# A decoder block on one core: self-attention's products, some copies and loads in another order

## What is computed

```python
# x: 4 x 512 x 128, ctx: 4 x 154 x 128, mask: 4 x 1 x 512 x 154
def attn(x, Wk, Wq, Wv):                      # one head of 128, causal
    scores = (x @ Wq) @ (x @ Wk)^T / sqrt(128), later keys at -inf
    return softmax(scores) @ (x @ Wv)

def xattn(q, kv, mask, ...):                  # 16 heads of 8, over the 154 rows of ctx
    scores = query @ key^T / sqrt(8), masked
    return (softmax(scores) @ value) @ wo + bo

def ffn(x, ...):                              # self-attention with rope, then experts
    q, k, v = x @ Wq + bq, x @ Wk + bk, x @ Wv + bv        # 16 heads of 8
    q, k = q * cos + rotate_half(q) * sin, k * cos + rotate_half(k) * sin
    ao = softmax(q @ k^T / sqrt(8)) @ v                    # 512 x 512 scores per head
    x1 = layernorm(x + ao @ Wo + bo) * g1 + be1
    p, i = top 2 of softmax(x1 @ Wg + bg) of 8 experts, p made to sum to 1
    y = sum of p * (gelu(x1 @ W1[i] + b1[i]) @ W2[i] + b2[i])   # hidden 512
    return layernorm(x1 + y) * g2 + be2

x = x + attn(layernorm(x), ...)
x = x + xattn(layernorm(x), ctx, mask, ...)
x = x + ffn(layernorm(x), ...)
```

## Time and profile before

| | us |
|---|---|
| median of 3 runs | 740.26 |
| lowest, highest | 740.03, 741.62 |
| the profiled execution | 746.73 |
| its span, first to last instruction | 744.9 |
| PE, DVE, ACT, POOL busy in the span | 645.0, 453.8, 344.4, 121.6 |

### The profile page before, as it was taken

One profiled execution on the slowest core, in us unless ns is written; L12 is line 12 of the kernel. 1 busy time (PEld: TensorE's weight loads), 2 busy tenths in 40 slices (PEclk: granted clock), 3 DMA queues, 4 the chain that ended last, 5 costly groups with the idle time before them and its releaser, 6 DMA issues.

```text
span 744.9 us, 10652 instructions
## 1 busy us (share of the span) xinstructions
PE 645.0 (87%) x3806; PEld 401.2 (54%) x3814; DVE 453.8 (61%) x1119; ACT 344.4 (46%) x617; POOL 121.6 (16%) x121
## 2 busy tenths in 40 slices
PE   4799899998898899999898899999888999886950
PEld 2563554456646653478536653388446643475950
DVE  4673777736836677467726578667534688377303
ACT  0405127663054567754235467754344476632620
POOL 5100100001143000010405100030406000224014
PEclk9999999999999999999899999999999999997985
DMA  6300000001053540012353430020354600126851
GB/s 193 109 0 1 1 0 1 1 1 36 4 176 95 143 110 1 1 35 80 101 153 84 131 99 1 1 76 18 102 149 125 170 20 0 29 65 201 255 143 42
DMA packets 45083, 54.95 MB, mean 74 GB/s; under 512 B 4346, under 2 KB 35432, under 8 KB 45032
## 3 DMA queue, kind: packets, MB, share of 16 engines
q1 hardware_dynamic: 43240, 50.61, 23.6%
q0 software_dynamic: 1792, 3.67, 1.6%
HBM read 46.73 MB, written 7.54 MB: 73 GB/s over the span
## 4 chain that ended last, share of the span: by engine, by line
PE 66%; DVE 18%; issue 5%; ACT 5%; DMA 2%; POOL 2%; SPq 1%; POOLq 0%; ACTq 0%; DVEq 0%
PE banks L1712 8%; PE banks L1680 6%; PE banks L1359 6%; PE banks L1373 5%; PE banks L1336 5%; PE banks L1702 4%; DVE nm L1192 3%; DVE nm L1128 3%; PE banks L1663 3%; PE banks L1607 2%; PE banks L1605 2%; PE banks L1624 2%; PE banks L1618 2%; DVE hat L886 1%; PE banks L1430 1%
## 5 line engine op out<-in xcount | busy, mean ns | idle before, releaser
L1192 DVE TENSOR_REDUCE nm<-banks 128x1 fp32r<-128x512 f32 x256 | 159.9, 684 | 43.4 <-PE banks L1680 43.2
L839 ACT ACTIVATE px<-banks 128x1024 f32<-128x1024 f32 x128 | 125.5, 1023 | 41.3 <-PE banks L1702 40.9
L667 ACT ACTIVATE hT<-banks,wp 128x128 f32<-128x128 f32 x240 | 68.3, 368 | 84.6 <-PE banks L1359 79.9
L559 POOL TENSOR_TENSOR rstd<-ve,misc 128x4 f32<-128x4 f32 x19 | 19.5, 1027 | 473.7 <-DVE ve L880 473.7
L1359 PE MATMUL banks<-xT,wp 128*128 128x128 f32 x480 | 70.0, 292 | 14.2 <-DMA wp<-in_experts 7.9
L1359 PEld LDWEIGHTS banks<-xT,wp 128*128 128x128 f32 x480 | 62.7, 203 | 21.0 <-issue 12.8
L1680 PE MATMUL banks<-kst,qst 32*128 32x512 f32 x256 | 70.7, 474 | 2.4 <-DVE nm L1192 1.4
L1373 PE MATMUL banks<-wp,hT 128*128 128x128 f32 x480 | 68.1, 288 | 2.1 <-ACT hT L667 2.1
L1712 PE MATMUL banks<-px,vf 128*32 128x512 f32 x512 | 68.2, 604 | 1.4 <-ACT px L839 0.7
L1336 PE MATMUL banks<-sel_r,eye_r 128*128 128x512 f32 x168 | 64.6, 463 | 5.0 <-DVE nm L1192 4.0
L1373 PEld LDWEIGHTS banks<-wp,hT 128*128 128x128 f32 x480 | 62.9, 203 | 3.6 <-ACT hT L667 2.6
(11 more groups left out here) (273 smaller groups left out, 997.5 us busy)
## 6 DMA issues: line engine op xcount, KB each, us to landing
wp<-in_experts SPq DMA_DIRECT2D x60, 514.0 KB
b2r<-in_L_ffn_b SPq DMA_DIRECT2D x60, 64.0 KB
expert_rows<-xs SPq DMA_DIRECT2D x12, 256.0 KB, 4.4
xs<-expert_tokens SPq DMA_DIRECT2D x9, 256.0 KB, 2.9
msk<-in_mask SPq DMA_DIRECT2D x4, 308.0 KB, 3.2
xin<-in_x SPq DMA_DIRECT2D x4, 256.0 KB, 2.9
ot<-in_const_sel SPq DMA_DIRECT2D x1, 1024.0 KB, 5.1
out<-yg SPq DMA_DIRECT2D x4, 256.0 KB, 2.4
```

What stands on the lines that cost most here:

```text
L667: ins = act.activation(hT[:, n % 2, c * P:(c + 1) * P], bank[h_bank(p, i)][:, c * P:(c + 1) * P], ACT.Gelu, bias=wp[:, n % WSLOTS, 2 * FF ...
L839: act.activation(px[:, c % 2, 2 * i:2 * i + 2, :], banks[:, 4 + 2 * i:6 + 2 * i, :], ACT.Exp, scale=SCALE_H).then_inc(k["f_exp"], 1)
L1192: dve.tensor_reduce(nm[:, t, g, BLK * hh:BLK * hh + 1], bank[s1_bank(g, t, hh)], AX.X, ALU.max, negate=True).then_inc(k["f_max"], 1)
```

## The change

1. Self-attention: the four `s1` of a query tile come in the order of heads 2, 3, 0, 1 (`HEADS_IN_TURN`), so that the two beside `s2` of heads 0 and 1 use the other rows of the array, and those beside `s2` of heads 2 and 3 too. The value sums move from behind the second `s2` to between the halves of a step (behind everything in a group's last step, or when no `s1` is left, which is as before for the latter). The keep-warm product before each `q2` is gone (16 in all).
2. Tail: VectorE normalises `xa` before the sum with o_proj, and makes klo before the moments of batch n (`keys_low`, split from `keys_values`); TensorE turns the rows before expert td, and makes the query projection before expert te; ScalarE's copies move with them (hatT before gelu td, qhi before gelu te). The query stacks of batches 2 and 3 get a wait for gelu te, whose bank they use.
3. `cross`: ScalarE copies khi before gelu w5b; TensorE's query stacks wait for qlo alone. The first token group is turned before the projection of the heads, with other `TURN_BANKS`, and the first `up` waits for two groups instead of four, the second for all.
4. SyncE: the last batch's first five experts are loaded before the last two stores of batch 2's expert rows, and no longer behind them.

```diff
@@ -114,9 +114,11 @@
 RING = 3
-RING_ORDER = [(0, t, hh) for t in range(T) for hh in range(HG)]
+
+HEADS_IN_TURN = (2, 3, 0, 1)
+RING_ORDER = [(0, t, i) for t in range(T) for i in range(HG)]
 for _g in range(G):
-    _next = [(_g + 1, t, hh) for t in range(T) for hh in range(HG) if _g + 1 < G]
+    _next = [(_g + 1, t, i) for t in range(T) for i in range(HG) if _g + 1 < G]
     RING_ORDER += _next[:2] + [(_g,)] + _next[2:]
@@ -131,7 +133,7 @@
 MISC = 256
-TURN_BANKS = (6, 5, 7, 6)
+TURN_BANKS = (5, 6, 7, 5)
 RANK_BANK = 6
@@ -510,15 +512,16 @@
             for p in range(B):
-                sp.wait_ge(k["g_eid"], p + 1)
-                for i in range(2):
-                    load_expert(p, i)
+                if p < B - 1:
+                    sp.wait_ge(k["g_eid"], p + 1)
+                    for i in range(2):
+                        load_expert(p, i)
                 if p < B - 1:
...
                         load_tokens(p, g)
-                for i in range(2, WSLOTS):
-                    load_expert(p, i)
+                    for i in range(2, WSLOTS):
+                        load_expert(p, i)
                 for i in range(WSLOTS, NT):
@@ -531,6 +534,10 @@
                 load_batch(p + 3)
+                if p == B - 2:
+                    sp.wait_ge(k["g_eid"], B)
+                    for i in range(WSLOTS):
+                        load_expert(B - 1, i)
                 for g in range((NT - WSLOTS) // YG, NG):
@@ -743,16 +750,16 @@
                     keys_high(n, 0)
-                if ahead:
-                    gelus(p - 1, "td")
-                if ahead:
-                    key_diagonals(n, 1)
                     act.wait_ge(k["ln_turned1"], n + 1)
...
                 if ahead:
+                    gelus(p - 1, "td")
+                if ahead:
+                    key_diagonals(n, 1)
+                if ahead:
+                    queries_high(n)
+                if ahead:
                     gelus(p - 1, "te")
-                if ahead:
-                    queries_high(n)
                 if after:
@@ -804,9 +811,9 @@
                 act.activation(qhi[:], rope_f[:, 0, :], ACT.Copy).then_inc(k["f_hi"], 1)
-                gelus(p, "w5b")
                 act.wait_ge(k["f_full"], 2 * n + 2)
                 act.activation(khi[:], rope_f[:, 1, :], ACT.Copy).then_inc(k["f_hi"], 1)
+                gelus(p, "w5b")
                 gelus(p, "w6")
@@ -935,10 +942,12 @@
 
-            def keys_values(n, i):
+            def keys_low(n, i):
                 dve.wait_ge(k["x_khi"], n + 1)
...
                                          khi[:, 0:KC], ALU.add, ALU.subtract).then_inc(k["x_klo"], 1)
+
+            def values(n, i):
                 dve.tensor_tensor(vx[:, :, 0:DH], bank[i][:, 160:160 + D].rearrange("p (h d) -> p h d", d=DH),
@@ -993,6 +1002,8 @@
                     add_biases(p - 1, "tc")
+                if ahead:
+                    ln_rows(1, n, xa, hat1, k["ln_hat1"])
                 if after:
@@ -1001,11 +1012,11 @@
                 if ahead:
-                    ln_rows(1, n, xa, hat1, k["ln_hat1"])
+                    keys_low(n, 0)
                 if after:
...
                 if ahead:
-                    keys_values(n, 0)
+                    values(n, 0)
                 if after:
@@ -1187,9 +1198,9 @@
                 def row_maxima(g, t):
-                    for hh in range(HG):
-                        dve.wait_ge(k["f_s1"], H * T * b + (g * T + t) * HG + hh + 1)
-                        dve.tensor_reduce(nm[:, t, g, BLK * hh:BLK * hh + 1], bank[s1_bank(g, t, hh)],
+                    for i, hh in enumerate(HEADS_IN_TURN):
+                        dve.wait_ge(k["f_s1"], H * T * b + (g * T + t) * HG + i + 1)
+                        dve.tensor_reduce(nm[:, t, g, BLK * hh:BLK * hh + 1], bank[s1_bank(g, t, i)],
                                           AX.X, ALU.max, negate=True).then_inc(k["f_max"], 1)
@@ -1335,8 +1347,8 @@
 
-            def turn_tokens(p):
-                for g in range(NG):
+            def turn_tokens(p, groups):
+                for g in groups:
                     pe.wait_ge(xs_in[g], 16 * (p + 1))
@@ -1350,8 +1362,8 @@
                     pe.wait_ge(k["xT_ready"], NG * p + i // YG + 1)
-                elif i == 0:
-                    pe.wait_ge(k["xT_ready"], NG * (p + 1))
+                elif i < 2:
+                    pe.wait_ge(k["xT_ready"], NG * p + (2, NG)[i])
                 if i:
@@ -1484,6 +1496,8 @@
                 for g in range(G):
+                    if n >= 2 and XQ_BANKS[g] in H_BANKS:
+                        pe.wait_ge(k["h_act"], NT * (n - 2) + gap_tiles("te").stop)
                     dst = bank[XQ_BANKS[g]]
@@ -1543,16 +1557,17 @@
                 if ahead:
+                    turn_rows(1, n, hat1, 4)
+                if ahead:
                     experts(p - 1, "td")
...
                     x_key_stacks(n, 1)
-                    turn_rows(1, n, hat1, 4)
-                if ahead:
-                    experts(p - 1, "te")
                 if ahead:
...
                     pe.matmul(bank[0], wx[:, 0, :], hatT[:], start=True, stop=True).then_inc(k["x_qproj"], 1)
+                if ahead:
+                    experts(p - 1, "te")
                 if after:
@@ -1642,9 +1657,11 @@
                 experts(p, "w2")
+                if p >= 0:
+                    turn_tokens(p, (0,))
                 project_heads(n, 0, wx[:, 3, :], 4)
                 if p >= 0:
-                    turn_tokens(p)
+                    turn_tokens(p, range(1, NG))
                 experts(p, "w3")
@@ -1654,8 +1671,9 @@
                 experts(p, "w5b")
-                pe.wait_ge(k["f_lo"], 2 * n + 2)
                 for i in range(4):
+                    if i % 2 == 0:
+                        pe.wait_ge(k["f_lo"], 2 * n + i // 2 + 1)
                     stack_part(n, 0, i)
@@ -1672,19 +1690,19 @@
                         else:
-                            g, t, hh = step
-                            pe.wait_ge(k["f_max"], H * T * b + (g * T + t) * HG + hh + 1)
-
-                def s1(g, t, hh):
-                    wait_slot(RING_ORDER.index((g, t, hh)))
-                    pe.matmul(bank[s1_bank(g, t, hh)], qst[blk(hh), g, t * P:(t + 1) * P], kst[blk(hh), g, :],
+                            g, t, i = step
+                            pe.wait_ge(k["f_max"], H * T * b + (g * T + t) * HG + i + 1)
+
+                def s1(g, t, i):
+                    hh = HEADS_IN_TURN[i]
+                    wait_slot(RING_ORDER.index((g, t, i)))
+                    pe.matmul(bank[s1_bank(g, t, i)], qst[blk(hh), g, t * P:(t + 1) * P], kst[blk(hh), g, :],
                               start=True, stop=True).then_inc(k["f_s1"], 1)
...
                     dst = bank[q2_bank(g)]
-                    keep_warm(1, q2_bank(g))
                     pe.matmul(dst, eye_r[:], qst[:, g, :], start=True, stop=False, skip_group_check=True)
@@ -1746,16 +1764,17 @@
                             s2(g, c, i)
-                            if i:
-                                if g * T + c == 1:
-                                    pe.wait_ge(k["f_v"], b + 1)
-                                if g * T + c:
-                                    sums_of(g * T + c - 1)
                             if ga < G:
...
                                 q2(g + 1)
+
+
+                            if g * T + c and i == (ga >= G or c == T - 1):
+                                if g * T + c == 1:
+                                    pe.wait_ge(k["f_v"], b + 1)
+                                sums_of(g * T + c - 1)
                             if g * T + c == 0:
```

11 lines of the change are left out of this document (6 added, 5 removed).

## The result

The changed kernel takes **730.1 us** (median of 4 runs, 727.8 to 733.9) where the kernel before takes 740.8 beside it: a ratio of 0.986, 95% interval 0.981 to 0.991. Measured again later it took 731.3 for 742.5 (0.985, 0.982 to 0.987). So 11 us are gained where 24.4 were forecast; 715.9 is missed by 14.2, and the range of 708 to 728 by 2. The profiled execution took 731.6, its span is 729.8. Ratios leave out executions more than 1.5% above the fastest of their kernel, medians do not, so the two can differ a little.

A forecast was written before the change was run, and what follows sets the result against it. Self-attention steps bound by TensorE's work (2.70 us) and an equally long dependence loop through VectorE's maxima (2.69). Terms 5.0 + 6.6 + 5.8 + 0 + 7.0 = 24.4 off span 744.9 give 720.5, less 6.5 gives 715.9 us; range 708 to 728.

The forecast's parts named there:

- the start of the sum: Whole kernel: profiled span 744.9 less 24.4 gives 720.5; the median's 6.5 us lower time, carried over, gives 715.9.
- the end: Last batch: weights loaded before the third batch's last row stores start expert 0 3.4 sooner; 7.0 us gained (3 to 9).
- the loop: Self-attention: new order of heads and sums, no keep-warm before q2; gain around the group's change, 5.0 us (2 to 8).
- the stacks: Before self-attention: khi before gelu w5b, query half waiting for qlo alone; 5.8 us of 6.5 gained (4 to 6.5).
- the tails: Batch tail with next cross-attention ahead: query stacks start 2.2 us sooner in each of three, 6.6 us (4 to 7.5).
- ordinary steps: Self-attention steps away from the group's change: forecast to stay at 2.70 us, held by the ring of three banks.
- B: Second of the four look-ahead s1 scores in a self-attention step; forecast to wait 0.41 us for its bank's maximum.
- The step behind the group's change: Self-attention, the step following a group's change: forecast to need only 2.28 us, 0.41 saved, given back one step later.
- Rival (b): Self-attention loop: four row tiles at once slower than two; 0.11 more a step, 720.7 us, 730.4 with no overlap; chance 0.05.
- rival (e): Self-attention loop: TensorE's clock falls to the low level, 1.9 us more a step; 16 such steps give 746.3; chance 0.03.
- First tokens: Cross-attention: first tokens turned before the projection, first expert behind two groups; forecast 0, TensorE only waits at another moment.
- Rival (a): Last batch: later stores move POOL's fetches, and these, not tile 7, release the final chain; no gain there, 722.9; chance 0.12.

The follow-up runs named there:

- b1: The changed kernel with the keep-warm product ahead of q2 put back; 0.989 (0.983 to 0.995) of the kernel before.
- e2: The kernel before with the self-attention loop's new order of heads and sums, keep-warm ahead of q2 kept; 0.9976 (0.9949 to 1.0002) of the kernel before.
- a1: The kernel before with only the self-attention loop's edits (heads 2 and 3 first, sums between halves, no keep-warm ahead of q2); 0.9989 of the kernel before.
- a4: The kernel before with only the last batch's first five experts loaded ahead of the third batch's last row stores; 0.9974 of the kernel before.

## Why the prediction was wrong, step by step

The miss of 14.2 us is, by the table and the medians: 5.0 the start of the sum, 4.1 the end, 2.5 low stretches, 1.4 the loop, 0.6 the stacks, 0.6 the opening, and 0.1 back from the tails.

**The start of the sum (5.0).** "The difference carried over gives 715.9": this failed. It takes the 6.5 us between profile and median for a constant that the changed kernel has too; its own was 1.5. 5.8 of the 6.5 were longer waits and low stretches at the start of self-attention of batches 2 and 3, which belong to that execution. Counted profile to profile, 24.4 would have been missed by 9.3 and not by 14.2. And the terms were read in it as if they were free of such things, which I never checked: 10.2 us of before's span were lost in low stretches and the waits beside them, outside the end.

**The loop (5.0).** Right in mechanism: ordinary steps stay at 2.74, TensorE waits about 0.4 before B, either edit alone is worse. Two sizes were off. The step behind the group's change was forecast at 2.28, TensorE's work, and takes 2.64: four maxima 0.60 apart need 2.40, a floor of VectorE's that I had not put beside it (the other 0.24 is not explained). The change itself takes 3.75 where I had 4.07, and the step that waits for `ot` 3.19 for 3.1. Without low stretches, 3.6 for 5.0. In the runs 0.8 is left (-1.0 to 2.5), and the low stretches can be the reason. Rival (b), row tiles slower together, did not happen: the four products of a half take 0.44, and an ordinary step is 2.74 for 2.70. The 3.07 for four row tiles that the prediction cited from the Trainium skill would have made it 2.83; the measurement decides.

**The clock, rival (e).** Given 0.03, with "slices with the loop show the full level everywhere" as the reason. A slice hides a stretch of 3.4 us, as said above, and those slices were of a loop in which TensorE was busy nearly all the time; the changed loop is another loop. The price per stretch was right in kind (1.45 measured at a step of 3.75, 1.9 estimated for one of 2.7), but I treated the case as all or nothing: 16 slow steps and a slower kernel. It came as two to five stretches a profile. The Trainium skill, page "TensorE: Matmul & The Clock Gate", section "A second HAM failure mode: psum-queue depth-cycling", says that short idle times between groups of matmuls can make the clock go back and forth. The traces agree, as far as they can: 25 low stretches in seven profiles of the new loop, 1 in five with a product added; but in b1 and e2 that product stands only ahead of q2 and the waits of 0.4 are as before, so that these waits do it is not shown.

**The tails (6.6) and stacks (5.8).** Right: 6.7 and 5.2 in the traces, 5.4 and 5.1 in the runs. Of the 6.5 us of waiting for klo, 1.0 belonged to that one execution (2.08 and 2.06 in batches 2 and 3; a1 and a4 wait 5.5 and 5.6 in all), hence 5.2.

**First tokens (0).** "TensorE only waits at another moment" was true, and wrong as a price: at this other moment, 1.7 in one piece behind a short burst of work, the low level begins 20 times of 24, and the edit alone is 4.6 us slower.

**The end (7.0, measured 2.9).** The forecast of TensorE's side was exact in a4 (expert 0 at 34.6); in the changed kernel's own profile it is 36.2, with the clock low ahead of it. The step that failed is "its start moves about 3 to 4 later against 8 gained, so I think it just fits": the fetches start 6.6 to 6.9 later, the second store goes 3.1 later, as I had it, but behind 2.9 MB of weights it then takes 6.4 us until the fetches start, and not 2.9. Tile 7's group was then not waited for at all; the third batch's sum was. Rival (a), given 0.12, is what happened.

The direction held (faster, given 0.95). The range failed at its upper end by 2 us: its bounds held the terms only, and neither the start of the sum nor (e) beside (a).

## What to carry to other kernels

Cut two traces at the same instructions and compare the pieces at full clock first: that gives what an edit does to 0.1 us, where the runs give it to 2. Take no time from one profiled execution without asking how much of its span was at the lower clock, by windows and not by the row of tenths, and how far it is from the median. Count waits that an edit moves or lengthens as risks of their own, also where they hide nothing. A product of no use that fits into a wait cost at most 0.1 us a loop and kept the later part of this loop at the full level, though the time gained by it stayed inside the noise. And where a transfer is moved ahead of another, follow the one that was passed to its last reader: here a store of rows, passed by five experts' weights, held back the output, and the output's store the last weights.

## What the runs showed of the hardware

- The time of one and the same program follows the mean granted clock from run to run, at about 0.4 us for each us at the low level where it spreads widely (0.18 to 0.26 for the kernel before where it does not). The spread differs by chip: 739 to 744 on two, 739 to 770 on two others, for the kernel before.
- A wait of 1.7 us on TensorE behind eight small products was followed by the low level 20 times of 24; at the same place without that wait it was so 0 times of 36.
- A low stretch can last while TensorE is busy all through it: in b1 from 567.7 for 17 us, of which the windows view has TensorE busy in all of the last 13.7.
- Two products of one pair of row tiles and two of another pair, 32 rows and 512 columns each, are through in 0.44 us, where one of 128 rows takes 0.42 (285.41 to 285.83).
- Pieces of the program without low stretches repeat to 0.1 us between kernels, runs and chips, but for the start of self-attention in batches 2 and 3, where the wide chips wait longer.
